# Seven-product gates of a graph recurrence: one part moved, one given its own bank, one load asked for sooner

## The chip, the core and the metric

The kernel runs on one core of one Trainium2 chip. The metric is the device time of one execution in microseconds, the median of several. TensorE (PE) multiplies and transposes into PSUM, used here as eight banks of 128 x 512 fp32; VectorE (DVE) and ScalarE (ACT) read the banks and work in SBUF; SyncE (SP) issues most DMAs. The engines run their own instruction lists in order and wait for each other by semaphores.

## The reference: what is computed

The first layer is a mean aggregation over a 2048 x 2048 adjacency with dense layers; the second is a recurrence of five steps over the same adjacency, cut to what matters:

```python
state = prop_state
for _ in range(N_STEPS):                       # 5
    s_in = state @ in_W.T + in_b
    s_out = state @ out_W.T + out_b
    a_in = Af @ s_in
    a_out = AfT @ s_out
    a = jnp.concatenate([a_in, a_out, state], axis=-1)
    r = jax.nn.sigmoid(a @ r_W.T + r_b)
    z = jax.nn.sigmoid(a @ z_W.T + z_b)
    joined = jnp.concatenate([a_in, a_out, r * state], axis=-1)
    h_hat = jnp.tanh(joined @ h_W.T + h_b)
    state = (1.0 - z) * state + z * h_hat
```

The state is 2048 nodes x 256 features.

## The kernel before

**Tiling and names.** The state lies transposed in `ST` as two feature tiles of 128 by 2048 nodes. Nodes are taken as two pairs of blocks of 512 nodes. One unit n is one pair in one step of the recurrence: n = -2 and -1 (`FIRST` and `FIRST + 1`) are the first and the second pair of step one, n = 0 and 1 those of step two, and so on to 7. u = n + 2 counts the units, p = n % 2 is the pair. The program runs for each n: from n = 0 on two product stages (x = 0, 1), then three gates j = 0 (r), 1 (z), 2 (h).

**Seven products.** The 2 x 2 block product of a gate (two feature tiles by two node blocks) is computed as seven products M1 to M7, called parts, each of three fp32 matmul steps of 128 x 128 by 128 x 512 (`part`); each step appears as two instructions in the trace, so a part is six. Four banks a, b, c, d serve a gate; a gate uses banks 0 to 3 or 4 to 7 in turn, as g = 5n + 2 + j is even or odd. Products accumulate on one another: M1 then M2 in a, M5 then M3 in c, M6 then M7 then M4 in b. Between them the engines take out what they need: ACT copies M1 (`m1_buf`) before M2 may be added, and M5 before M3; DVE adds the bias terms to the tiles of `buf` (two scalar_tensor_tensor for one tile, a pair, L1282 and L1285, `add_bias`), reads M6 out of b (L1295) before M7, and M6 + M7 (`u3`, L1306) before M4. The semaphore `part_ready` counts the parts done (7 per gate), `part_act` ACT's two copies, `part_dve` nine DVE steps per gate (the third is the sum of M6, the ninth u3), `value_ready` the four finished tiles. ACT squashes each tile when its value is ready (L908). After the values of gate 0 DVE multiplies r by the state (L1239, `reset_times_state`), in gate 1 it forms four reset sums (L1214 to L1219, `reset_sums`, semaphore `reset_ready`), which gate 2 waits for.

**Order of the parts.** In most gates PE runs M1, M5, M6, M2, M7, M3, M4 (`GATE`). For the gate n = -1, j = 0 the order is written out apart (`LATE`): M1, M5, M2, M3, transposes, M6, M7, M4, because its sums XT2 to XT4 of the right-hand sides are made late by DVE (`first_sums`, L1161 to L1164).

**Fresh leaves.** In gate 0 of a second pair PE transposes the first pair's new state into the four banks of the gate before (`turn_fresh`, 16 transposes, L489). ACT copies three of them and writes their fp16 high parts (`leaf_first`, L739), DVE forms the low parts (`leaf_low`, L1135, called splits here) and four sums (`leaf_sums`, L1117 to L1122), and ACT the high parts of these. Gate 1 of the same unit writes into the banks which the transposes used, and so waits for `leaf_act` and `leaf_sum`. DVE's order in this gate: bias of tile 1; M6; bias of tiles 3, 2, 0; three splits; u3; tile 2; leaf sums; M3 into tile 1; four splits; two r times state; M4 into tile 3.

**Streamed blocks.** From n = 0 on `product` multiplies fp16 leaves (`LF`) by adjacency blocks of 1 MB, which SP loads from `quad_d` in the order `LOADS` (M1, M6, M5, M2, M7, M3, M4) into six slots. The first three are requested early. Block 3 (M2 of n = 0) and all behind it are requested after `node_ready` has reached 8, the last new state of n = -1. Slot 3 lies at 120 KB, where `first_XS` lies, the state sums that the third matmul step of gates 0 and 1 reads in the first two units. In the first products (x = 0, p = 0) the order on PE is M1, half of M6, half of M5, M2, the other halves, M7, M3, M4, with leaf transposes between them; each product is 16 matmuls, each half 8.

Of the kernel before, what the change touches and what calls it, by code (L numbers as in the profile page):

```python
# [8 lines left out]
ALU = mybir.AluOpType  # L9
# [14 lines left out]
M1, M2, M3, M4, M5, M6, M7 = range(7)  # L24
PLAIN = (M1, M6, M5, M2, M7, M3, M4)
EARLY = (M1, M2, M6, M5, M7, M3, M4)
LATE = (M1, M5, M2, M3, M6, M7, M4)
GATE = (M1, M5, M6, M2, M7, M3, M4)
FIRST = -2
LOADS = (M1, M6, M5, M2, M7, M3, M4)  # L30
# [14 lines left out]
def graph_net(nc, x, adj, w_in, w_out, wg_t, w0_t, w_comb, w_o, cols, b_comb, o2_b, consts, out):  # L45

    ctx = ExitStack()
    with ctx:
# [3 lines left out]
        def sem(name):  # L52
            return ctx.enter_context(nc.semaphore(name))
# [139 lines left out]
        value_ready, squashed = sem("value_ready"), sem("squashed")  # L193
        rs2_ready, kept_ready = sem("rs2_ready"), sem("kept_ready")
        own_ready, reset_ready = sem("own_ready"), sem("reset_ready")
        moved, node_ready = sem("moved"), sem("node_ready")
        leaf_ready, leaf_act, leaf_sum = sem("leaf_ready"), sem("leaf_act"), sem("leaf_sum")
        leaf_hi, leaf_lo = sem("leaf_hi"), sem("leaf_lo")
# [42 lines left out]
        def _(sp):  # L241
# [52 lines left out]
            for k in range(14 * 2 * (STEPS - 1)):  # L294
                n, y, i = k // 14, k // 7 % 2, k % 7
                if k == 3:
                    sp.wait_ge(node_ready, 8)
                if k >= SLOTS:
                    o = k - SLOTS
                    sp.wait_ge(prod_ready, 7 * (o // 7) + place(o // 14, o // 7 % 2, LOADS[o % 7]) + 1)  # L300
                sp.dma_start(slot[k % SLOTS][:, :, :], quad_d[y, n % 2, LOADS[i]]).then_inc(ld_slot[k % SLOTS], 16)
# [20 lines left out]
        def _(pe):  # L322
            ident = cst[:, C_ID:C_ID + P]

            def mm(o, l, r, start, stop, again=False):
                return pe.matmul(o, l, r, start=start, stop=stop, skip_group_check=again)  # L326
# [231 lines left out]
            def gate_group(n, j, last_step):  # L558
# [14 lines left out]
                    third = {M1: r_state[:, 0, :], M2: r_state[:, 3, :], M3: r_state[:, 2, :],  # L573
                             M4: rt4[:, :], M5: r_state[:, 1, :], M6: rt2[:, :], M7: rt3[:, :]}

                def part(op, o):
                    for k in range(FT):
                        mm(o[:, :], W7[:, op, j, k, :], right[op][:, k, :], k == 0 and op in (M1, M5, M6), False, True)
                    mm(o[:, :], W7[:, op, j, 2, :], third[op], False, True, True).then_inc(part_ready, 1)

                def turn_fresh():
# [34 lines left out]
                if n == FIRST + 1 and j == 0:  # L616
                    part(M1, a)
                    pe.wait_ge(own_ready, 4 * u + 4)
                    part(M5, c)
                    pe.wait_ge(part_act, 2 * done + 1)  # L620
                    part(M2, a)
                    pe.wait_ge(part_act, 2 * done + 2)
                    part(M3, c)
                    turn_fresh()
                    pe.wait_ge(x_ready, 4 * u + 2)
                    part(M6, b)
                    pe.wait_ge(x_ready, 4 * u + 4)
                    pe.wait_ge(part_dve, PARTS * done + AT_U2)
                    part(M7, b)
                    pe.wait_ge(part_dve, PARTS * done + AT_U3)  # L630
                    part(M4, b)
                    return
                part(M1, a)
                if j == 0:
# [297 lines left out]
        def _(dve):  # L932
# [327 lines left out]
            def gate_group(n, j, last_step):  # L1260
                p = n % 2
                g = 5 * n + 2 + j
                a, b, c, d = half_banks(g)
                done = 3 * (n - FIRST) + j
                buf = bufs_of(n)[j]
                m1, u3 = m1_buf[:, g % 2, :], u3_buf[:, :]
                n1 = slice(2 * p * BN, 2 * p * BN + BN)
                n2 = slice((2 * p + 1) * BN, (2 * p + 1) * BN + BN)
                fresh_here = j == 0 and p == 1 and not last_step
                tail = j == 2 and p == 1 and not last_step  # L1270
                parts = [PARTS * done]

                def step(ins):
                    parts[0] += 1
                    ins.then_inc(part_dve, 1)

                def own_wait():
                    dve.wait_ge(part_dve, parts[0])

                def add_bias(o, i, f, nodes):  # L1280
                    t = 2 * j + f
                    step(v.scalar_tensor_tensor(out=o, in0=degA_all[:, nodes], scalar=gcol[:, 0, t:t + 1],  # L1282
                                                in1=i, op0=ALU.mult, op1=ALU.add))
                    own_wait()
                    return v.scalar_tensor_tensor(out=o, in0=degT_all[:, nodes], scalar=gcol[:, 1, t:t + 1],  # L1285
                                                  in1=o, op0=ALU.mult, op1=ALU.add)

                def ready(op):
                    dve.wait_ge(part_ready, 7 * done + gate_place(n, j, op) + 1)

                dve.wait_ge(part_act, 2 * done + 1)
                step(add_bias(buf[:, 1, :], m1, 0, n2))
                ready(M6)
                own_wait()
                step(v.tensor_tensor(buf[:, 1, :], b[:, :], buf[:, 1, :], ALU.add))  # L1295
                assert parts[0] == PARTS * done + AT_U2
                step(add_bias(buf[:, 3, :], m1, 1, n1))
                dve.wait_ge(part_act, 2 * done + 2)
                step(add_bias(buf[:, 2, :], buf[:, 2, :], 1, n2))
                ready(M2)  # L1300
                add_bias(buf[:, 0, :], a[:, :], 0, n1).then_inc(value_ready, 1)
                if fresh_here:
                    leaf_low(n + 1, 0, 3)
                ready(M7)
                own_wait()
                step(v.tensor_tensor(u3, b[:, :], m1, ALU.add))  # L1306
                assert parts[0] == PARTS * done + AT_U3 == PARTS * (done + 1)
                own_wait()
                v.tensor_tensor(buf[:, 2, :], u3, buf[:, 2, :], ALU.add).then_inc(value_ready, 1)
                if j == 1:  # L1310
                    reset_sums(n)
                if fresh_here:
                    leaf_sums(n + 1, half_banks(g - 1)[3])
                if j == 2:
                    renew(n, 0)
                ready(M3)
                v.tensor_tensor(buf[:, 1, :], c[:, :], buf[:, 1, :], ALU.add).then_inc(value_ready, 1)
                if fresh_here:
                    leaf_low(n + 1, 3, 7)
                if j == 0:  # L1320
                    reset_times_state(n, 0, 2)
                if j == 2:
                    renew(n, 1)
                if tail:
                    leaf_low(n + 2, 0, 1)
                if n == FIRST and j == 2:
                    own_sums(n + 1)
                ready(M4)
                v.tensor_tensor(buf[:, 3, :], b[:, :], buf[:, 3, :], ALU.add).then_inc(value_ready, 1)
                if j == 2:  # L1330
                    renew(n, 2)
                    renew(n, 3)
                if n == FIRST and j == 2:
                    first_sums(n + 1)
# [97 lines left out]
```

## Time and profile before

| | |
|---|---|
| median of 3 runs | 1252.18 us (1252.12 to 1252.78) |
| profiled execution | 1251.93 us, span 1250.1 us |
| granted TensorE clock, mean | 0.994 |
| TensorE | 1226.1 us busy, 98% of the span |
| VectorE | 761.6 us, 61% |
| ScalarE | 286.9 us, 23% |
| blocks streamed into the slots | 112 of 1024 KB, median 5.1 us to landing |

The span is the time from the first to the last instruction of the profiled execution. Idle time of an engine counts only where it lies on the chain of work that ends last. That chain is 88% TensorE.

### The profile page before, as it was taken

The page shows a single profiled execution, that of the slowest core. Times are in us where ns is not written, and L with a number is a line of the kernel's source. Part 1 is how long each engine was busy: PE and PEld are TensorE (multiplying, and loading weights), DVE is VectorE, ACT ScalarE, POOL GpSimd, SP SyncE. Part 2 cuts the span into 40 slices and gives each one's busy share as a digit, 9 for nine tenths or more (in the row PEclk, how much of TensorE's full clock was granted, in tenths as well). Part 3 has the DMA queues.
Part 4 walks back from the last instruction along what each step waited for, and adds up shares of the span by engine and source line. Part 5 has one row for each costly group of instructions (what it writes and reads, how often), then busy time and mean ns, then how long its engine had stood idle before and what let it go on. Part 6 is the DMA issues. An engine that isn't in the chain of part 4 may idle for free.

```text
span 1250.1 us, 12880 instructions
## 1 busy us (share of the span) xinstructions
PE 1226.1 (98%) x4886; PEld 596.3 (48%) x4886; DVE 761.6 (61%) x1276; ACT 286.9 (23%) x556; POOL 3.0 (0%) x9
## 2 busy tenths in 40 slices
PE   7999999999899999999999999999999999999998
PEld 5666654444344444444444444444444444444445
DVE  5677662796876366278537438735734863662674
ACT  4755300012223012022202103311211330120121
POOL 0000000000000000000000000000000000000000
PEclk9899999999999999999999999999999999999999
DMA  8454460980004911830560480083076029116202
GB/s 307 140 169 164 185 270 37 353 323 1 1 0 190 345 38 48 305 118 0 224 247 1 147 304 21 34 298 139 1 247 224 1 85 352 35 40 229 89 1 68
DMA packets 44506, 180.61 MB, mean 144 GB/s; under 512 B 3489, under 2 KB 13474, under 8 KB 29346
## 3 DMA queue, kind: packets, MB, share of 16 engines
q1 hardware_dynamic: 43440, 176.04, 39.0%
q0 software_dynamic: 720, 3.67, 0.8%
q8 instruction: 36, 0.59, 0.2%
q14 instruction: 20, 0.16, 0.0%
q10 hardware_dynamic: 290, 0.14, 0.0%
HBM read 144.71 MB, written 35.13 MB: 144 GB/s over the span
## 4 chain that ended last, share of the span: by engine, by line
PE 88%; DVE 1%; issue 0%; ACT 0%; DVEq 0%
PE bank L326 86%; PE bank L489 1%; DVE LF L1135 0%; DVE GR L1282 0%; PE bank L442 0%; DVE GR L1285 0%; DVE H L1040 0%; PE bank L395 0%; DVE DR L1008 0%; DVE AT L997 0%; DVE fresh_S L1119 0%; DVE fresh_L L1117 0%; DVE GR L1295 0%; DVE res L1393 0%; DVE stat L947 0%
## 5 line engine op out<-in xcount | busy, mean ns | idle before, releaser
L326 PE MATMUL bank<-slot,LF 128*128 128x512 f16 x1792 | 389.5, 379 | 1.7 <-DVE LF L1135 1.7
L326 PEld LDWEIGHTS bank<-slot,LF 128*128 128x128 f16 x1792 | 175.1, 98 | 212.2 <-issue 4.4
L326 PE MATMUL bank<-X,W 128*128 128x512 f32 x384 | 180.5, 592 | 0.0
L326 PE MATMUL bank<-XT,W 128*128 128x512 f32 x288 | 135.3, 592 | 0.0
L326 PEld LDWEIGHTS bank<-X,W 128*128 128x128 f32 x384 | 72.5, 190 | 88.0 <-issue 86.8
L326 PE MATMUL bank<-AT,SN 128*128 (+1 forms) x256 | 97.1, 379 | 0.0
L326 PE MATMUL bank<-A,SN 128*128 (+1 forms) x256 | 97.0, 379 | 0.0
L1181 DVE TENSOR_TENSOR u_buf<-bank,m_buf 128x512 f32<-128x512 f32 x16 | 11.1, 691 | 134.0 <-PE bank L326 134.0
L326 PEld LDWEIGHTS bank<-XT,W 128*128 128x128 f32 x288 | 54.7, 190 | 68.9 <-issue 68.2
L739 ACT ACTIVATE m_buf<-bank 128x512 f32<-128x512 f32 x46 | 27.4, 595 | 232.0 <-PE bank L326 232.0
L326 PE MATMUL bank<-DR,work 128*128 128x512 f16 x256 | 65.7, 379 | 3.0 <-DVE DR L1008 3.0
L326 PE MATMUL bank<-XS,W 128*128 128x512 f32 x128 | 65.4, 592 | 0.0
L326 PE MATMUL bank<-ST,W 128*128 128x512 f32 x120 | 61.3, 592 | 0.0
L908 ACT ACTIVATE GR<-GR,col 128x512 f32<-128x512 f32 x40 | 28.8, 721 | 99.7 <-DVE GR L1285 54.0
L326 PE MATMUL bank<-first_X,W 128*128 128x512 f32 x96 | 45.3, 594 | 0.0
L908 ACT ACTIVATE GZ<-GZ,col 128x512 f32<-128x512 f32 x32 | 23.1, 722 | 85.6 <-DVE GZ L1285 55.3
L908 ACT ACTIVATE GH<-GH,col 128x512 f32<-128x512 f32 x32 | 23.1, 722 | 85.5 <-DVE GH L1285 56.4
L326 PE MATMUL bank<-GR,W 128*128 128x512 f32 x80 | 40.9, 592 | 0.0
L326 PE MATMUL bank<-first_XT,W 128*128 128x512 f32 x72 | 35.8, 621 | 4.7 <-DVE u_buf L1306 3.8
L739 ACT ACTIVATE A<-WG 128x512 f16<-128x512 int32 x64 | 39.5, 620 | 0.3 <-DMA WG<-in_adj 0.2
L326 PEld LDWEIGHTS bank<-A,SN 128*128 (+1 forms) x256 | 25.0, 98 | 29.9
L326 PEld LDWEIGHTS bank<-AT,SN 128*128 (+1 forms) x256 | 25.0, 98 | 29.7
(209 smaller groups left out, 1412.5 us busy)
## 6 DMA issues: line engine op xcount, KB each, us to landing
slot<-quad_d SPq DMA_DIRECT2D x112, 1024.0 KB, 5.1
WG<-in_adj SPq DMA_DIRECT2D x32, 512.0 KB, 4.2
quad_d<-AT SPq DMA_DIRECT2D x12, 1024.0 KB, 5.0
quad_d<-A SPq DMA_DIRECT2D x12, 1024.0 KB, 9.5
quad_d<-spare SPq DMA_DIRECT2D x4, 1024.0 KB, 4.0
SN<-in_x SPq DMA_DIRECT2D x2, 1024.0 KB, 10.4
x_d<-SN POOLq DMA_DIRECT2D x4, 512.0 KB, 2.9
x1o<-x_d SPq DMA_DIRECT2D x1, 2048.0 KB, 8.1
```

The source lines that it names most:

```text
L326: return pe.matmul(o, l, r, start=start, stop=stop, skip_group_check=again)
L489: last = pe.transpose(o[:, q * P:q * P + P], ST[:, f, n0:n0 + P], ident)
L739: return nc.scalar.activation(o, i, ACT.Copy, scale=scale, **kw)
L908: nc.scalar.activation(buf[:, tile, :], buf[:, tile, :], ACT.Tanh if j == 2 else ACT.Sigmoid, bias=col[:, 10 + 2 * j + f:11 + 2 * j + f]). ...
L1181: v.tensor_tensor(u3, b[:, :], m1, ALU.add).then_inc(prod_dve, 1)
```

## The change

In the gate n = -1, j = 0 the part M3 is issued between M6 and M7 instead of ahead of the transposes, and M4 goes into bank d with a start flag of its own. M7 waits for eight DVE steps instead of three, the eighth being the sum of M6; M4 waits for no DVE step. DVE does the bias additions of tiles 3, 2 and 0 ahead of the sum of M6, does the leaf sums before it waits for M7, adds the products of M7 to tile 3 (one more instruction, semaphore `late_sum`), and adds M4 from bank d. In SP's list block 3 waits for 35 parts, that is, for the end of gate 1 of n = -1, and block 4 for `node_ready` 8. All other gates and units keep their order.

```diff
--- before.py
+++ after.py
@@ -24,7 +24,7 @@
 M1, M2, M3, M4, M5, M6, M7 = range(7)
 PLAIN = (M1, M6, M5, M2, M7, M3, M4)
 EARLY = (M1, M2, M6, M5, M7, M3, M4)
-LATE = (M1, M5, M2, M3, M6, M7, M4)
+LATE = (M1, M5, M2, M6, M3, M7, M4)
 GATE = (M1, M5, M6, M2, M7, M3, M4)
 FIRST = -2
 LOADS = (M1, M6, M5, M2, M7, M3, M4)
@@ -193,6 +193,7 @@
         value_ready, squashed = sem("value_ready"), sem("squashed")
         rs2_ready, kept_ready = sem("rs2_ready"), sem("kept_ready")
         own_ready, reset_ready = sem("own_ready"), sem("reset_ready")
+        late_sum = sem("late_sum")
         moved, node_ready = sem("moved"), sem("node_ready")
         leaf_ready, leaf_act, leaf_sum = sem("leaf_ready"), sem("leaf_act"), sem("leaf_sum")
         leaf_hi, leaf_lo = sem("leaf_hi"), sem("leaf_lo")
@@ -294,6 +295,8 @@
             for k in range(14 * 2 * (STEPS - 1)):
                 n, y, i = k // 14, k // 7 % 2, k % 7
                 if k == 3:
+                    sp.wait_ge(part_ready, 7 * 5)
+                if k == 4:
                     sp.wait_ge(node_ready, 8)
                 if k >= SLOTS:
                     o = k - SLOTS
@@ -573,9 +576,10 @@
                     third = {M1: r_state[:, 0, :], M2: r_state[:, 3, :], M3: r_state[:, 2, :],
                              M4: rt4[:, :], M5: r_state[:, 1, :], M6: rt2[:, :], M7: rt3[:, :]}
 
-                def part(op, o):
+                def part(op, o, alone=False):
                     for k in range(FT):
-                        mm(o[:, :], W7[:, op, j, k, :], right[op][:, k, :], k == 0 and op in (M1, M5, M6), False, True)
+                        mm(o[:, :], W7[:, op, j, k, :], right[op][:, k, :],
+                           k == 0 and (alone or op in (M1, M5, M6)), False, True)
                     mm(o[:, :], W7[:, op, j, 2, :], third[op], False, True, True).then_inc(part_ready, 1)
 
                 def turn_fresh():
@@ -619,16 +623,15 @@
                     part(M5, c)
                     pe.wait_ge(part_act, 2 * done + 1)
                     part(M2, a)
-                    pe.wait_ge(part_act, 2 * done + 2)
-                    part(M3, c)
                     turn_fresh()
                     pe.wait_ge(x_ready, 4 * u + 2)
                     part(M6, b)
+                    pe.wait_ge(part_act, 2 * done + 2)
+                    part(M3, c)
                     pe.wait_ge(x_ready, 4 * u + 4)
-                    pe.wait_ge(part_dve, PARTS * done + AT_U2)
+                    pe.wait_ge(part_dve, PARTS * done + PARTS - 1)
                     part(M7, b)
-                    pe.wait_ge(part_dve, PARTS * done + AT_U3)
-                    part(M4, b)
+                    part(M4, d, True)
                     return
                 part(M1, a)
                 if j == 0:
@@ -1288,33 +1291,48 @@
                 def ready(op):
                     dve.wait_ge(part_ready, 7 * done + gate_place(n, j, op) + 1)
 
+                def products_of(op):
+                    return {M2: a, M3: c, M4: d if late else b, M6: b, M7: b}[op][:, :]
+
+                late = n == FIRST + 1 and j == 0
                 dve.wait_ge(part_act, 2 * done + 1)
                 step(add_bias(buf[:, 1, :], m1, 0, n2))
+                if late:
+                    step(add_bias(buf[:, 3, :], m1, 1, n1))
+                    dve.wait_ge(part_act, 2 * done + 2)
+                    step(add_bias(buf[:, 2, :], buf[:, 2, :], 1, n2))
+                    ready(M2)
+                    add_bias(buf[:, 0, :], products_of(M2), 0, n1).then_inc(value_ready, 1)
                 ready(M6)
                 own_wait()
-                step(v.tensor_tensor(buf[:, 1, :], b[:, :], buf[:, 1, :], ALU.add))
-                assert parts[0] == PARTS * done + AT_U2
-                step(add_bias(buf[:, 3, :], m1, 1, n1))
-                dve.wait_ge(part_act, 2 * done + 2)
-                step(add_bias(buf[:, 2, :], buf[:, 2, :], 1, n2))
-                ready(M2)
-                add_bias(buf[:, 0, :], a[:, :], 0, n1).then_inc(value_ready, 1)
+                step(v.tensor_tensor(buf[:, 1, :], products_of(M6), buf[:, 1, :], ALU.add))
+                if not late:
+                    assert parts[0] == PARTS * done + AT_U2
+                    step(add_bias(buf[:, 3, :], m1, 1, n1))
+                    dve.wait_ge(part_act, 2 * done + 2)
+                    step(add_bias(buf[:, 2, :], buf[:, 2, :], 1, n2))
+                    ready(M2)
+                    add_bias(buf[:, 0, :], products_of(M2), 0, n1).then_inc(value_ready, 1)
                 if fresh_here:
                     leaf_low(n + 1, 0, 3)
+                if late:
+                    leaf_sums(n + 1, half_banks(g - 1)[3])
                 ready(M7)
                 own_wait()
-                step(v.tensor_tensor(u3, b[:, :], m1, ALU.add))
+                step(v.tensor_tensor(u3, products_of(M7), m1, ALU.add))
                 assert parts[0] == PARTS * done + AT_U3 == PARTS * (done + 1)
                 own_wait()
                 v.tensor_tensor(buf[:, 2, :], u3, buf[:, 2, :], ALU.add).then_inc(value_ready, 1)
+                if late:
+                    v.tensor_tensor(buf[:, 3, :], products_of(M7), buf[:, 3, :], ALU.add).then_inc(late_sum, 1)
                 if j == 1:
                     reset_sums(n)
-                if fresh_here:
+                if fresh_here and not late:
                     leaf_sums(n + 1, half_banks(g - 1)[3])
                 if j == 2:
                     renew(n, 0)
                 ready(M3)
-                v.tensor_tensor(buf[:, 1, :], c[:, :], buf[:, 1, :], ALU.add).then_inc(value_ready, 1)
+                v.tensor_tensor(buf[:, 1, :], products_of(M3), buf[:, 1, :], ALU.add).then_inc(value_ready, 1)
                 if fresh_here:
                     leaf_low(n + 1, 3, 7)
                 if j == 0:
@@ -1326,7 +1344,9 @@
                 if n == FIRST and j == 2:
                     own_sums(n + 1)
                 ready(M4)
-                v.tensor_tensor(buf[:, 3, :], b[:, :], buf[:, 3, :], ALU.add).then_inc(value_ready, 1)
+                if late:
+                    dve.wait_ge(late_sum, 1)
+                v.tensor_tensor(buf[:, 3, :], products_of(M4), buf[:, 3, :], ALU.add).then_inc(value_ready, 1)
                 if j == 2:
                     renew(n, 2)
                     renew(n, 3)
```

## Rows read from the trace of the kernel before

**Rows 1.** The page: TensorE busy over the whole span.

```profile
PE 1226.1 (98%) x4886; PEld 596.3 (48%) x4886; DVE 761.6 (61%) x1276; ACT 286.9 (23%) x556; POOL 3.0 (0%) x9
```

**Rows 2.** Waits of PE, 316 to 420: line, waited for, us, times, longest.

```profile
PE bank L326 <- DVE u_buf L1306: 3.8, 1, 3.8
PE bank L326 <- DVE LF L1135: 1.7, 1, 1.7
PE bank L326 <- DVE GR L1295: 0.9, 1, 0.9
```

**Rows 3.** Timeline 316 to 350: start us, us, engine, line, operation, out<-in, count.

```profile
320.38 1.88 PE L326 MATMUL bank<-first_X,W 128*128 128x512 f32 x4
...
328.10 1.88 PE L326 MATMUL bank<-first_X,W 128*128 128x512 f32 x4
...
329.45 0.75 DVE L1282 SCALAR_TENSOR_TENSOR GR<-DR,gcol,m_buf 128x512 f32<-128x512 f16 x1
...
332.42 1.88 PE L326 MATMUL bank<-first_XT,W 128*128 128x512 f32 x4
...
335.20 0.69 DVE L1295 TENSOR_TENSOR GR<-bank,GR 128x512 f32<-128x512 f32 x1 [4.22 <-PE bank L326]
...
335.81 0.74 DVE L1282 SCALAR_TENSOR_TENSOR GR<-DR,gcol,m_buf 128x512 f32<-128x512 f16 x1
...
336.04 1.96 PE L326 MATMUL bank<-first_XT,W 128*128 128x512 f32 x4 [0.88 <-DVE GR L1295]
...
340.15 1.89 DVE L1135 SCALAR_TENSOR_TENSOR LF<-fresh_L,LF 128x512 f16<-128x512 f32 x3
...
342.69 3.78 PE L326 MATMUL bank<-first_XT,W 128*128 128x512 f32 x4 [3.84 <-DVE u_buf L1306]
...
343.28 0.68 DVE L1117 TENSOR_TENSOR fresh_L<-bank,fresh_L 128x512 f32<-128x512 f32 x1
...
346.53 0.68 DVE L1135 SCALAR_TENSOR_TENSOR LF<-fresh_S,LF 128x512 f16<-128x512 f32 x1
```

**Rows 4.** Timeline 346 to 384, gate j = 1.

```profile
347.97 2.05 PE L326 MATMUL bank<-first_X,W 128*128 128x512 f32 x4
...
350.14 0.68 DVE L1329 TENSOR_TENSOR GR<-bank,GR 128x512 f32<-128x512 f32 x1
...
351.49 0.58 ACT L739 ACTIVATE m_buf<-bank 128x512 f32<-128x512 f32 x1
...
352.22 0.75 DVE L1282 SCALAR_TENSOR_TENSOR first_GZ<-DR,gcol,m_buf 128x512 f32<-128x512 f16 x1
...
361.22 0.69 DVE L1306 TENSOR_TENSOR u_buf<-bank,m_buf 128x512 f32<-128x512 f32 x1
...
364.61 0.68 DVE L1219 TENSOR_TENSOR RT<-GR,first_RT 128x512 f32<-128x512 f32 x1
...
366.17 1.88 PE L326 MATMUL bank<-first_X,W 128*128 128x512 f32 x4
```

**Rows 5.** Stretches: length, PE busy, the other engines, granted clock, DMA share, GB/s.

```profile
336.00:339.00 3.00, 2.81 (x6) 1.06 (x6) 2.93 (x5) 0.00 (x0) 0.00 (x0) 1.00 0.00 0
...
339.00:342.00 3.00, 0.00 (x0) 0.00 (x0) 2.96 (x6) 0.72 (x1) 0.00 (x0) 0.91 0.00 0
...
343.00:346.00 3.00, 3.00 (x4) 1.20 (x4) 2.93 (x6) 2.00 (x4) 0.00 (x0) 0.50 0.00 0
```

**Rows 6.** Timeline 388 to 398; landing times of the blocks requested.

```profile
389.92 1.99 SPq L301 DMA_DIRECT2D slot<-quad_d  x4
...
391.28 1.89 PE L326 MATMUL bank<-slot,LF 128*128 128x512 f16 x8
...
394.85 3.40 PE L326 MATMUL bank<-slot,LF 128*128 128x512 f16 x15 [1.68 <-DVE LF L1135]
...
DMA to landing us min/median/max: 4.8/7.9/10.9
```

**Rows 7.** Timeline 592 to 612, the same products one step later.

```profile
601.62 10.74 PE L326 MATMUL bank<-slot,LF 128*128 128x512 f16 x49
```

## The prediction, made before the changed kernel was run

> **What bounds the kernel now.** I read the page first: TensorE is busy 1226 us of a span of 1250 [rows 1], so a change pays only where it takes idle or slow time from TensorE. The waits of TensorE around the change are three [rows 2]: 3.8 us for the vector engine's u3 (L1306), 1.7 us put down to a leaf split (L1135), 0.9 us for the sum of M6 (L1295). The timeline [rows 3, 4] shows where they lie. In the first gate of the second pair (n = -1, j = 0; M1 starts at 320.38) three parts take 328.10 - 320.38 = 7.72 us, 2.573 each; the 16 transposes follow M3 and end 1.74 us later, at 332.42, where M6 starts. At 336.04 M7 starts, 1.05 us after M6 gave TensorE free (332.42 + 2.57 = 334.99). M7 is issued by 338.61, and M4 starts at 342.69, 4.08 us late. M4 then takes 347.97 - 342.69 = 5.28 instead of 2.57, since the granted clock is 0.50 there (the 1.2 GHz level), having fallen in the 3.84 us of idleness [rows 5]. The next gate (j = 1) takes 366.17 - 347.97 = 18.20 us for seven parts worth 18.01, the last 0.19 of the low clock. So 1.05 + 4.08 + 2.71 + 0.19 = 8.0 us lie here beyond the matmuls' own time, and about 1.8 more lie at the first products.
>
> **The sequence after the change, TensorE up to M7.** M1, M5 and M2 keep their places and end at 328.10. M3 leaves, so the transposes run from 328.10 to 329.84, M6 to 332.42 (DVE writes its operand XT2 ahead of the bias additions, which start at 329.45, [rows 3]), M3 to 334.99. The transposes need the first pair's new states, finished before those additions as well. Nothing is paid for this exchange, it fills the time that DVE needs.
>
> **VectorE up to M7.** The additions start at 329.45 as before. In the row, three pairs take 340.15 - 335.81 = 4.34 us, 1.447 a pair [rows 3]. Now four pairs stand in a row ahead of the sum of M6: 329.45 + 4 x 1.447 = 335.24. M6 itself is ready at about 332.6, so the sum is held by VectorE and starts at 335.24, practically where it did before (335.20). From that sum's start to M7 is 336.04 - 335.20 = 0.84, so M7 starts at 336.08, a wait of 1.09 us, 0.04 more than now. The gap at M7 is not removed.
>
> **M4 in bank d.** It no longer waits for u3. It starts at 336.08 + 2.57 = 338.65 and ends at 341.22. That takes away the 4.08 us, and, as no long gap is left, the 2.71 + 0.19 of the low clock. The trace shows no M4 that opens a bank; M1 opens one in each gate and costs the same 2.57, so I take nothing for it (bounds: 0 to the 0.04 by which my part lengths are uncertain). At the end of the gate the gain is 347.97 - 341.22 = 6.75 us.
>
> **What VectorE now has in front of the next gate.** Nothing of its work went away and one addition came (tile 3 plus the products of M7, 0.61 us by the step 335.20 to 335.81). Three leaf splits take 1.89; the four leaf sums 2.65 (343.28 to 346.53 holds five instructions, less one of 0.61) [rows 3]. So: sum of M6 335.24, splits 335.85, leaf sums from 337.77, when the last split is done, to 340.5 (337.77 + 2.65 and 0.07 of a last instruction's end). Gate j = 1 writes the banks that the transposes used and waits for these sums; TensorE comes at 341.22, 0.7 later, so nothing is paid. u3 starts at 340.4, value 1 at 341.1, the new addition 341.75, the sum of M3 342.4. The next four splits wait for ScalarE: a sigmoid and a copy of some 0.6 to 0.7 us each (351.49 - 350.14 - 0.68 is 0.67, the copy itself 0.58, [rows 4]) behind value 1, so 343.15. From that split to the sum of M4 is 350.14 - 346.53 = 3.61: 346.8, where M4 was ready long before (341.4). That is 5.6 us behind the start of j = 1; now it is 350.14 - 347.97 = 2.2. VectorE is late by 3.4 us relative to TensorE, and this is where a new wait can come.
>
> **Gate j = 1.** The sum of M4 to the copy of M1 is 351.49 - 350.14 = 1.35: the copy ends at 346.8 + 1.35 + 0.58 = 348.7. TensorE wants it for M2 at 341.22 + 3 x 2.573 = 348.94: free by 0.2. The first addition starts 352.22 - 350.14 = 2.08 behind the sum of M4, at 348.9, the sum of M6 at 350.35, M7 could start at 351.2 and its turn is 351.5: free by 0.3. Three pairs and a step later, 350.35 + 0.61 + 4.34 = 355.3, u3 starts and ends at 356.0; M4's turn is 356.66: free. The last of the reset sums ends 364.61 + 0.68 - 361.22 = 4.07 behind u3's start [rows 4], at 359.35; j = 2 waits for it, and its turn is 341.22 + 18.01 = 359.23. Here 0.1 to 0.2 us of waiting appear, where now 0.9 are free (365.29 against 366.17). I take j = 2 at 359.45; the bounds are 359.23 and, if each of VectorE's handovers costs 0.1 more, 359.95. Gain at that point: 366.17 - 359.45 = **6.7 us** (6.2 to 6.9). In j = 2 VectorE waits for matmuls again, so no lag is carried on.
>
> **The fourth block.** At the first products (n = 0) the half of M5 starts at 391.28 and M2 at 394.85 [rows 6]. Eight matmuls of 0.216 are 1.73, so M2 is 1.84 us late. The wait is put down to L1135, but the code of M2 wants the leaf splits up to the tenth, which is that of L12, and not the later one, of a leaf sum, that ended just before 394.85; and in the next step the same sequence runs 49 matmuls without a gap from 601.62, with the same leaf chain beside it [rows 7]. What differs here is block 3, requested at 389.92, when the state is ready, and the quickest of these transfers took 4.8 us to land: 394.72. So it is the block. Asked for after 35 parts, that is at the end of j = 1 (about 359.4, slot 3 being the bytes of first_XS, whose last reader is that M4), it has some 23 us until 383 (389.92 less the gain of 6.7), more to M2. It lands beneath j = 2; SP has nothing else to request until the state is ready, and the DMA share is 0.00 in each stretch of [rows 5]. On SP's queue only the wait for block 4 stands behind it, whose condition comes 24 us later. Block 4 becomes the first of the burst; M7 wants it two products after M2's turn, so about 393.0 + 6.9 = 399.9 on the old clock, against a landing near 394.7. What is late next are the leaf splits of M6's second half: 394.83 against the end of M2 at 393.01 + 3.45 = 396.46, free by 1.6. Gain **1.84 us** (bounds 0, if it were the split after all, and 1.84).
>
> **Sum.** 6.7 + 1.84 = 8.55 us. Behind that the chain is TensorE alone, so it arrives in full. The profiled execution took 1251.93 us (span 1250.1, 1.8 around it); it becomes 1243.4, span 1241.55. It lies 0.25 below the median of the runs, 1252.18, so I forecast a median of **1243.6**.
>
> **Rivals.**
> 1. **The load is not the limit at M2** (the split is). Then only 6.7 come: 1245.5. For it speaks the releaser named in rows 2, against it the step-two sequence. Chance 0.05.
> 2. **The clock falls in the gap before M7.** The gap of 1.09 us stays. If the clock fell there, M7 and M4 would run at 0.50, as M4 does now, for the 2.7 + 0.2 us that it costs now: 1246.5. Against it: the same gap of 1.05 us with the same matmuls before it left the clock at 1.00 in 336:339, and it fell only in the idle stretch of 339:342 [rows 5]. Chance 0.05. The Trainium skill, "TensorE: Matmul & The Clock Gate", Part 4: PE-mode transpose, says that transposes don't count as busy in the way that matmuls do; and its section A second HAM failure mode: psum-queue depth-cycling says that small idle gaps between groups that cycle through banks can make the clock oscillate. Both speak against this order, which has transposes, a gap and one more bank; by them the time would be this rival's. The trace speaks for less: before the change the transposes lie nearer to that gap and the clock held.
> 3. **VectorE is the bound of j = 1 and j = 2** rather than a neighbour: the lag of 3.4 us costs 0.2 to 0.5 at M2, M7 and at the start of j = 2 together some 1 us: 1244.6. For it speaks that its queue is full from 329.45 on, against it that each of my margins is positive but one. Chance 0.09.
> 4. **Slower than before.** The clock falls before M7 and stays low, since the gates keep having small gaps (M2, M7, the start of j = 2). Each matmul instruction at half speed costs 0.43 us more, so 20 of them beyond the saving, some 17 us at the low clock, eat the 8.55; past that it is slower. If it held for j = 1 and j = 2 whole it would be 36 - 8.6 = 27 us slower, 1280. In the rows now it was back for nearly all of j = 1, which took 18.20 us instead of 18.01, so 0.01.
>
> The forecast has 0.80. **Range**: the bounds of the terms give 8.77 to 8.0, 1243.4 to 1244.2; with rivals 1 and 3 and 0.7 for the scatter of the runs (1252.12 to 1252.78) it is 1242.6 to 1246.0. This kernel's measurement can tell about 0.2%, 2.5 us, from no change. Faster by more than that 0.98 (all cases but the last and mixtures of them), within it 0.01, slower 0.01.
>
> **What would show it.** M4 right behind M7 and the clock at 1.00 through 340 to 350; M7 still about 1.1 us late, released by L1295 (or its new line); start of j = 1 at 341.2, of j = 2 at 359.4 with a small wait for L1219; block 3 issued near 359.4 and M2 of n = 0 without a gap. Wrong would be a larger gap at M7 (the additions taking more than 1.45 a pair against the copies), a clock at 0.50 in that stretch, or a gap at M2 of n = 0 with the block landed.

## The result

The changed kernel takes **1244.37 us** (median of four runs, 1243.72 to 1245.34) against 1252.15 before (1251.26 to 1252.78): ratio 0.9939, 95% interval 0.9922 to 0.9956. The forecast was 1243.6, range 1242.6 to 1246.0. The profiled execution took 1245.34 us, span 1243.5. Run again on another occasion, five times beside nine runs of the kernel before, the two stood at 1245.46 and 1253.37, ratio 0.9940 (0.9927 to 0.9954).

The page's line on the engines, the answer to [rows 1]: TensorE is busy for 1.6 us less and the span is shorter by 6.6, so most of the gain is idle time.

```profile
PE 1224.5 (98%) x4886; PEld 596.1 (48%) x4886; DVE 762.2 (61%) x1277; ACT 286.3 (23%) x556; POOL 3.0 (0%) x9
```

The waits of TensorE between 316 and 420 us (line, waited for, us in total, times, longest), the answer to [rows 2]:

```profile
PE bank L329 <- DVE GR L1308: 0.9, 1, 0.9
PE bank L329 <- DVE RT L1222: 0.2, 1, 0.2
```

The long wait for u3 (3.8) and the one at the first products (1.7) are gone, the one of 0.9 us at M7 stays, and a new one of 0.2 us for the last reset sum has come. In the timeline of the changed kernel, which answers [rows 3, 4] (start us, us, engine, line, operation):

```profile
322.06 1.88 PE L329 MATMUL bank<-first_X,W 128*128 128x512 f32 x4
...
331.14 0.74 DVE L1285 SCALAR_TENSOR_TENSOR GR<-DR,gcol,m_buf 128x512 f32<-128x512 f16 x1
...
336.93 0.68 DVE L1308 TENSOR_TENSOR GR<-bank,GR 128x512 f32<-128x512 f32 x1
...
337.76 1.96 PE L329 MATMUL bank<-first_XT,W 128*128 128x512 f32 x4 [0.91 <-DVE GR L1308]
...
340.41 1.88 PE L329 MATMUL bank<-first_XT,W 128*128 128x512 f32 x4
...
342.18 0.68 DVE L1322 TENSOR_TENSOR u_buf<-bank,m_buf 128x512 f32<-128x512 f32 x1
...
342.99 1.88 PE L329 MATMUL bank<-first_X,W 128*128 128x512 f32 x4
...
348.52 0.68 DVE L1349 TENSOR_TENSOR GR<-bank,GR 128x512 f32<-128x512 f32 x1
...
351.38 0.75 DVE L1288 SCALAR_TENSOR_TENSOR first_GZ<-H,gcol,first_GZ 128x512 f32<-128x512 f16 x1
...
352.24 0.69 DVE L1308 TENSOR_TENSOR first_GZ<-bank,first_GZ 128x512 f32<-128x512 f32 x1
...
357.19 0.68 DVE L1322 TENSOR_TENSOR u_buf<-bank,m_buf 128x512 f32<-128x512 f32 x1
...
360.57 0.69 DVE L1222 TENSOR_TENSOR RT<-GR,first_RT 128x512 f32<-128x512 f32 x1
...
361.40 1.95 PE L329 MATMUL bank<-first_X,W 128*128 128x512 f32 x4 [0.22 <-DVE RT L1222]
```

M7 starts at 337.76, M4 stands right behind it at 340.41, while u3 (L1322) starts only at 342.18, and the next gate starts at 342.99. The gate j = 2 starts at 361.40.

To compare executions, I count from the first matmul of M1 in the gate n = -1, j = 0, at 320.38 before and at 322.06 here, since up to there both kernels issue the same work:

| from the gate's first matmul, us | before | changed | forecast |
|---|---|---|---|
| M7 | 15.66 | 15.70 | 15.70 |
| M4 | 22.31 | 18.35 | 18.27 |
| gate j = 1 | 27.59 | 20.93 | 20.84 |
| gate j = 2 | 45.79 | 39.34 | 39.07 |
| last instruction | 925.67 | 917.45 | 917.12 |

(The last instruction starts at 1246.05 before and 1239.51 now.) So the change is worth 8.22 us. The profiled execution shows 6.6 because it came to the gate 1.68 us later. That difference is older than the change, in the start of the kernel. The stretch 40 to 50 us, before and then changed (length, busy us of PE, PEld, DVE, ACT, POOL, granted clock, DMA share, GB/s):

```profile
40.00:50.00 10.00, 10.00 (x99) 5.93 (x99) 5.80 (x19) 8.72 (x29) 0.00 (x0) 1.00 0.67 214
```

```profile
40.00:50.00 10.00, 9.98 (x85) 5.71 (x86) 5.01 (x16) 7.54 (x25) 0.00 (x0) 0.83 0.57 184
```

A clock of 0.83 over ten us is 1.7 us of work not done. It goes with the execution and not with the change: among the profiles of the experiments below, the kernel before with M3 moved has 0.86 in this stretch and the changed kernel with late leaf sums 1.00. The nine runs of before of the second occasion fit this: four lie at 1252.0 to 1252.4 with mean clocks of 0.994 and 0.995, five at 1253.4 to 1253.9 with 0.992 and 0.993, and none between.

The granted clock in the gate, which answers [rows 5]:

```profile
336.00:339.00 3.00, 2.09 (x5) 0.70 (x5) 2.96 (x6) 0.72 (x1) 0.00 (x0) 1.00 0.00 0
...
339.00:342.00 3.00, 3.00 (x8) 1.33 (x7) 2.83 (x5) 0.00 (x0) 0.00 (x0) 1.00 0.00 0
...
342.00:345.00 3.00, 3.00 (x8) 1.33 (x7) 2.85 (x6) 1.38 (x3) 0.00 (x0) 1.00 0.00 0
```

It stays at 1.00 (2.4 GHz) over the gap of 0.91 us and behind it; before it fell to 0.50 (1.2 GHz) in the idle stretch ahead of M4.

At the first products, the answer to [rows 6], and the request of block 3:

```profile
361.21 0.32 SPq L304 DMA_DIRECT2D slot<-quad_d  x1
...
385.23 1.27 SPq L304 DMA_DIRECT2D slot<-quad_d  x3
...
386.58 5.78 PE L329 MATMUL bank<-slot,LF 128*128 128x512 f16 x26
...
389.44 0.68 DVE L1138 SCALAR_TENSOR_TENSOR LF<-fresh_S,LF 128x512 f16<-128x512 f32 x1
```

The half of M5 and M2 behind it are one row of matmuls from 386.58 on, with no gap. M2 starts at 386.58 + 8 x 0.216 = 388.31, a microsecond before the split L1138, to which the wait was put down before, even begins (389.44). SP requests three blocks here instead of four; the fourth was requested at 361.21, when the last part of j = 1 was done.

### The profile page after: what moved, and what is told of

Its sections match the earlier page's. It is cut to its first block, busy times and chain, and to the rows that moved or that the text cites. A ratio compares the mean times of both kernels' runs of the same rounds, so it can differ in the third digit from the quotient of the medians.

```text
span 1243.5 us, 12882 instructions
## 1 busy us (share of the span) xinstructions
PE 1224.5 (98%) x4886; PEld 596.1 (48%) x4886; DVE 762.2 (61%) x1277; ACT 286.3 (23%) x556; POOL 3.0 (0%) x9
## 4 chain that ended last, share of the span: by engine, by line
PE 85%; DVE 3%; issue 1%; ACT 0%; DVEq 0%
PE bank L329 84%; PE bank L492 1%; DVE LF L1138 0%; DVE GR L1285 0%; DVE first_GZ L1285 0%; DVE first_GH L1258 0%; DVE first_GZ L1288 0%; DVE GR L1288 0%; DVE ST L1261 0%; DVE u_buf L1322 0%; DVE GR L1242 0%; PE bank L445 0%; ACT GR L911 0%; DVE H L1043 0%; DVE first_XT L1166 0%
## 5 line engine op out<-in xcount | busy, mean ns | idle before, releaser
L329 PEld LDWEIGHTS bank<-XS,W 128*128 128x128 f32 x128 | 24.3, 190 | 30.6 <-issue 30.6
```

## The experiments

The experiments are compared by the distances from the gate's first matmul, which repeat to 0.05 us in four kernels that were profiled twice, where medians of four to ten runs scatter by one (the changed kernel profiled a second time: 15.71, 18.36, 20.94, 39.36 and 917.49).

| kernel | M7 | M4 | j = 1 | j = 2 | last | median, ratio to the kernel before as run beside it (interval) |
|---|---|---|---|---|---|---|
| before | 15.66 | 22.31 | 27.59 | 45.79 | 925.67 | |
| changed | 15.70 | 18.35 | 20.93 | 39.34 | 917.45 | 1244.37, 0.9939 (0.9922 to 0.9956) |
| changed, late request | 15.71 | 18.36 | 20.94 | 39.35 | 919.31 | 1246.93, 0.9949 (0.9932 to 0.9965) |
| before, early request | 15.66 | 22.32 | 27.60 | 45.68 | 923.74 | 1250.47, 0.9983 (0.9973 to 0.9992) |
| changed, M4 in bank b | 15.70 | 20.86 | 25.23 | 43.26 | 921.31 | 1249.04, 0.9964 (0.9950 to 0.9978) |
| changed, M3 in its old place | 15.71 | 18.36 | 20.94 | 39.36 | 917.48 | 1244.84, 0.9937 (0.9920 to 0.9954) |
| changed, leaf sums late | 15.71 | 18.36 | 23.37 | 43.16 | 921.22 | 1247.57, 0.9958 (0.9941 to 0.9974) |
| before, M3 moved | 14.62 | 19.74 | 23.21 | 41.31 | 921.21 | 1248.40, 0.9967 (0.9956 to 0.9979) |
| changed, sum of M6 sooner | 14.62 | 17.20 | 20.64 | 39.63 | 917.77 | 1245.58, 0.9940 (0.9923 to 0.9957) |
| less ahead of the next gate | 14.63 | 17.20 | 19.78 | 37.93 | 915.99 | 1243.33, 0.9926 (0.9910 to 0.9943) |

### The request of block 3, undone and alone

```diff
-                if k == 3:
-                    sp.wait_ge(part_ready, 7 * 5)
-                if k == 4:
+                if k == 3:
                     sp.wait_ge(node_ready, 8)
```

> The changed kernel, but block 3 is requested behind the last new state again, as before the change. Times are counted from the first matmul of M1 in the gate n = -1, j = 0 (changed kernel: j = 2 starts at 39.34, last instruction at 917.45; before: 45.79 and 925.67). Theory (the landing of block 3 releases M2 of the first products): M2 waits again, 1.8 us, last instruction at 919.2, some 0.14% slower than the changed kernel. Rival (the leaf split releases it, and the change of order removed that): no wait, 917.45.

Measured: 919.31, 1.86 more than the changed kernel; up to j = 2 nothing differs. The wait is back, and put down to the split again (first products of this kernel):

```profile
385.21 2.08 SPq L302 DMA_DIRECT2D slot<-quad_d  x4
...
386.57 1.89 PE L327 MATMUL bank<-slot,LF 128*128 128x512 f16 x8
...
389.43 0.68 DVE L1136 SCALAR_TENSOR_TENSOR LF<-fresh_S,LF 128x512 f16<-128x512 f32 x1
...
390.12 2.10 PE L327 MATMUL bank<-slot,LF 128*128 128x512 f16 x9 [1.66 <-DVE LF L1136]
...
DMA to landing us min/median/max: 4.8/7.9/10.9
```

The order of splits, transposes and products is that of the changed kernel, only the request is later: 385.21 + 4.8 = 390.0, and M2 starts at 390.12. The split ends at 390.11 by chance. In the changed kernel M2 did not wait for it, so it is the block.

> The kernel before with the early request alone. Theory: j = 2 starts at 45.79 as before, M2 of the first products follows the half of M5 without a gap, last instruction at 925.67 - 1.84 = 923.8. Rival (the split): 925.67, the wait stays and is released by the same split.

The other way round (the two lines of the change alone put into the kernel before): 923.74, 1.93 less, of which 0.11 was there before j = 2 starts (45.68 for 45.79; the clock was back a little sooner in j = 1). The request is worth 1.8 us with either order of the gate. Both expectations of the theory hold, the rival falls.

### M4 in bank b again

```diff
-                    part(M4, d, True)
+                    pe.wait_ge(part_dve, PARTS * done + AT_U3)
+                    part(M4, b)
...
-                return {M2: a, M3: c, M4: d if late else b, M6: b, M7: b}[op][:, :]
+                return {M2: a, M3: c, M4: b, M6: b, M7: b}[op][:, :]
...
-                if late:
-                    v.tensor_tensor(buf[:, 3, :], products_of(M7), buf[:, 3, :], ALU.add).then_inc(late_sum, 1)
...
-                if late:
-                    dve.wait_ge(late_sum, 1)
```

> The changed kernel, but M4 goes on in bank b behind u3, and the addition of M7 to tile 3 is gone. Theory: u3 ends 20.8 after the gate's start, M4 starts at 20.85 instead of 18.35 (a gap of 2.5 us), j = 1 at 23.4, and as TensorE is then behind VectorE, j = 2 at 41.5: 2.1 us over the changed kernel if the clock stays at 1.00 in a gap of 2.5 us. Rival (the clock falls in this gap as it did in 4.1 us): M4 takes up to 5.3 us, 5 us over the changed kernel, so that the own bank was worth most of the gain by the clock alone.

Measured: M4 at 20.86, as expected, but j = 1 at 25.23, j = 2 at 43.26, last 921.31: 3.86 us over the changed kernel, neither 2.1 nor 5. The timeline of TensorE and the clock around it:

```profile
337.81 1.96 PE L329 MATMUL bank<-first_XT,W 128*128 128x512 f32 x4 [0.92 <-DVE GR L1309]
...
342.97 3.28 PE L329 MATMUL bank<-first_XT,W 128*128 128x512 f32 x4 [2.34 <-DVE u_buf L1323]
...
346.04 1.46 PE L329 MATMUL bank<-first_XS,W 128*128 128x512 f32 x2
...
347.34 1.88 PE L329 MATMUL bank<-first_X,W 128*128 128x512 f32 x4
```

```profile
341.00:343.00 2.00, 0.03 (x1) 0.03 (x1) 1.94 (x4) 0.00 (x0) 0.00 (x0) 1.00 0.00 0
...
343.00:345.00 2.00, 2.00 (x3) 0.91 (x4) 1.29 (x3) 1.33 (x3) 0.00 (x0) 0.63 0.00 0
...
345.00:347.00 2.00, 2.00 (x4) 0.77 (x3) 2.00 (x4) 2.00 (x4) 0.00 (x0) 0.52 0.00 0
```

M4 took 347.34 - 342.97 = 4.37 instead of 2.57: the clock fell behind a gap of 2.34 us (1.00 in 341 to 343, then 0.63 and 0.52), which my theory had not expected, and it was low for less long than in the kernel before. So the bank alone is worth 3.9 us: 2.5 of waiting and 1.8 of clock, less 0.4 of waiting at j = 2 that is not needed then. Profiled again, it gave 20.86, 25.21, 43.23 and 921.30:

> M4 in bank b, again, for its clock around the gap of 2.34 us, where it fell. Theory (differs between executions): 921.3 from the gate's first matmul to the last instruction, or down to 919.5 with the clock at 1.00. Rival (fixed by the order of work, here two gaps in a row): 921.3 again.

It is the same to 0.03, though this execution came to the gate 1.53 us sooner (320.58 for 322.11). The rival of this run holds in these two executions: the fall and its price come with the order of work. Its moment does not: in the first execution M4 starts at 342.97 and the clock is still 1.00 in 343.0 to 343.5 and 0.51 in 343.5 to 344.0; in the second M4 starts at 341.44 and the clock is 0.92 in 341.0 to 341.5 and 0.50 in 341.5 to 342.0, so it fell as M4 started, half a microsecond sooner.

### M3 in its old place

```diff
                     part(M2, a)
+                    pe.wait_ge(part_act, 2 * done + 2)
+                    part(M3, c)
                     turn_fresh()
                     pe.wait_ge(x_ready, 4 * u + 2)
                     part(M6, b)
-                    pe.wait_ge(part_act, 2 * done + 2)
-                    part(M3, c)
```

(`LATE` with it.)

> The changed kernel, but M3 stands ahead of the transposes again. Theory (the sum of M6 starts when the four pairs of additions are done, and M6 is ready before that in either order): M6 ends 14.6 after the gate's start, the sum starts at 14.87, M7 at 15.70 as in the changed kernel, total the same within 0.1 us. Rival (M3 behind M6 is what covers the wait for the sum): M7 starts up to 2.5 us later, total 1 to 2.5 us longer.

Measured: 15.71 and 917.48, the theory to 0.03. In the changed kernel the move of M3 brings nothing, since all four pairs of additions stand ahead of the sum of M6 anyway, and M7 waits for them in either order.

### Leaf sums behind u3 again

```diff
-                if late:
-                    leaf_sums(n + 1, half_banks(g - 1)[3])
                 ready(M7)
...
-                if fresh_here and not late:
+                if fresh_here:
                     leaf_sums(n + 1, half_banks(g - 1)[3])
```

> The changed kernel, but the leaf sums come behind u3 and its two additions again. Times from the first matmul of M1 in the gate n = -1, j = 0. Theory: u3 starts at 18.55 (when M7 is done), the leaf sums run from 20.5 to 23.2, j = 1 waits for them and starts at 23.25 instead of 20.93, j = 2 at about 41.3 instead of 39.34: 2 us over the changed kernel. Rival (the next gate is released by something else, and VectorE has the same work in either order): j = 2 within 0.5 us of 39.34.

Measured: j = 1 at 23.37 (expected 23.25), so it is these sums that the next gate waits for; but j = 2 at 43.16, 3.8 us over the changed kernel instead of 2. The gate j = 1 took 43.16 - 23.37 = 19.79 where its parts need 18.02. The waits of this kernel, and its clock behind them:

```profile
PE bank L329 <- DVE fresh_L L1125: 2.3, 1, 2.3
PE bank L329 <- DVE GR L1308: 0.9, 1, 0.9
```

```profile
343.00:345.00 2.00, 1.17 (x3) 0.68 (x4) 2.00 (x5) 2.00 (x5) 0.00 (x0) 1.00 0.00 0
...
345.00:347.00 2.00, 2.00 (x3) 0.67 (x2) 2.00 (x4) 0.19 (x1) 0.00 (x0) 0.50 0.00 0
```

The clock fell again, this time 1.2 us after TensorE had gone on (343.83), to 0.50 in 345 to 347, behind idle stretches of 0.92 and 2.27 us. The theory named the right release, but it put the price at 2 us, about half of what was measured, because it left out the clock.

### M3 moved alone in the kernel before

The edit of the fourth kernel the other way round, in the kernel before.

> The kernel before with M3 moved between M6 and M7 alone (M4 in bank b, additions behind the sum of M6, late request). Theory: the sum of M6 runs under M3, M7 starts at 14.6 without a gap, u3 ends at 19.7, M4 starts at 19.75 with a gap of 2.6 us; with the clock at 1.00 the gate j = 1 starts at 23.1 (behind the leaf sums), j = 2 at 41.2, last instruction at 921.1, 4.6 under the kernel before. Rival (the clock falls in a gap of 2.6 us): some 2.9 us more, 924.0.

Measured: M7 at 14.62 without a gap, M4 at 19.74, j = 1 at 23.21, j = 2 at 41.31, last 921.21. The theory holds throughout, and the clock stayed at 1.00 although the gap is 2.38 us, longer than the two behind which it fell:

```profile
336.52 1.88 PE L326 MATMUL bank<-first_XT,W 128*128 128x512 f32 x4
...
341.64 1.98 PE L326 MATMUL bank<-first_XT,W 128*128 128x512 f32 x4 [2.38 <-DVE u_buf L1306]
...
345.11 1.96 PE L326 MATMUL bank<-first_X,W 128*128 128x512 f32 x4 [0.63 <-DVE fresh_L L1122]
```

```profile
339.00:341.00 2.00, 0.26 (x1) 0.00 (x0) 2.00 (x5) 0.72 (x1) 0.00 (x0) 1.00 0.00 0
...
341.00:343.00 2.00, 1.36 (x3) 0.68 (x4) 1.93 (x4) 0.65 (x1) 0.00 (x0) 1.00 0.00 0
...
343.00:345.00 2.00, 1.48 (x4) 0.38 (x2) 1.97 (x4) 1.40 (x4) 0.00 (x0) 1.00 0.00 0
```

> M3 moved alone, again, for its clock in the gap of 2.38 us ahead of M4, where it stayed at 1.00. Theory (whether the clock falls in a gap of about 2.3 to 2.4 us differs between executions of one kernel): the last instruction lies 921.2 behind the gate's first matmul, or up to 3.6 more. Rival (it is fixed by the kernel's order of work): 921.2 again.

Again: 19.75, 23.22, 41.32, 921.22, the clock at 1.00. Both executions came to the gate at nearly the same moment (321.90 and 321.97), so the two alone don't exclude that the moment decides. The times of the seven runs do: the profiled one took 1248.94 with the gate at 321.90, that is 5.83 beyond 321.90 + 921.21, and the two shortest, 1247.57 and 1247.66, then put the gate at about 320.5 if the clock held. Had it fallen there, at a price of 1.8, the gate would have come at 318.8, and no profile here has it before 320.38. What differs from the two kernels where it fell is what TensorE did before the gap: here it was unbroken up to it, there it had been idle for 0.92 us one or two parts earlier. That this earlier gap is what tips it is the reading that fits; no run changes it alone.

So the same move that is worth nothing in the changed kernel is worth 4.5 us alone (925.67 - 921.21): M4 starts 2.57 us sooner, the gate needs 3.47 us from there instead of 5.28, since the clock stays up, and j = 1 takes 18.10 instead of 18.20.

### The gap at M7, taken away

```diff
                 if late:
                     step(add_bias(buf[:, 3, :], m1, 1, n1))
-                    dve.wait_ge(part_act, 2 * done + 2)
-                    step(add_bias(buf[:, 2, :], buf[:, 2, :], 1, n2))
-                    ready(M2)
-                    add_bias(buf[:, 0, :], products_of(M2), 0, n1).then_inc(value_ready, 1)
                 ready(M6)
...
                 step(v.tensor_tensor(buf[:, 1, :], products_of(M6), buf[:, 1, :], ALU.add))
+                if late:
+                    dve.wait_ge(part_act, 2 * done + 2)
+                    step(add_bias(buf[:, 2, :], buf[:, 2, :], 1, n2))
+                    ready(M2)
+                    add_bias(buf[:, 0, :], products_of(M2), 0, n1).then_inc(value_ready, 1)
```

M7 waits for step 5 instead of step 8.

> The changed kernel, but VectorE takes the sum of M6 behind two pairs of additions instead of four, so that it runs under M3. Theory (VectorE's queue, not the gap at M7, sets the start of j = 2): M7 starts at 14.6, the gap of 1.1 us is gone, j = 1 waits for the leaf sums until 20.4, and j = 2 starts at 39.3 to 39.6, no sooner than in the changed kernel: total the same or 0.2 longer. Rival (what TensorE gains stays gained): j = 2 at 38.3, 1.05 us less.

Measured: M7 at 14.62, the gap of 1.08 us gone, and j = 2 at 39.63, 0.29 later than in the changed kernel; last 917.77. Its waits show where the 1.08 us went:

```profile
PE bank L329 <- DVE fresh_L L1125: 0.7, 1, 0.7
PE bank L329 <- DVE RT L1222: 0.3, 1, 0.3
```

j = 1 starts 0.87 us later than M4's end would allow (17.20 + 2.57 = 19.77 against 20.64), and from j = 1 to j = 2 it is 18.99 us where 18.02 are the parts' own: 0.97 lost, against 0.39 in the changed kernel. All of the 1.08 is given back, and 0.3 more. Of the 0.97 us, 0.51 are ahead of j = 2 and 0.29 ahead of M2 of j = 1, which starts at 350.83 behind ScalarE's copy of M1 (ended at 350.78); the rest is in the first instructions behind the gaps. The 0.3 are VectorE's own: it now waits 0.18 us for M6, and its splits start at 15.75 (337.86) instead of 15.47 (337.53). The theory holds, with sizes a little short (20.4 and at most 39.6 were expected). VectorE's queue from the additions to the last reset sum is the bound: in the changed kernel it is busy for 29.1 of these 30.1 us, and its one wait for another engine is 0.19 us, for a sigmoid of ScalarE. A gap of TensorE inside it costs nothing as long as the clock holds.

### Less of VectorE's work ahead of the next gate

On top of the kernel before this one: the splits and leaf sums stand ahead of the pairs of tiles 2 and 0, and behind the reset sums of j = 1 go two of the late splits and the addition of u3 to tile 2.

```diff
+                if j == 1 and n == FIRST + 1:
+                    reset_sums(n)
                 v.tensor_tensor(buf[:, 2, :], u3, buf[:, 2, :], ALU.add).then_inc(value_ready, 1)
...
-                    leaf_low(n + 1, 3, 7)
+                    leaf_low(n + 1, 3, 5 if late else 7)
+                if j == 1 and n == FIRST + 1:
+                    leaf_low(n + 1, 5, 7)
```

> As the run before, and VectorE has less ahead of the start of j = 2: leaf splits and sums before the last two pairs, two of the four late splits and the tile addition of u3 in j = 1 behind the reset sums. Theory (VectorE's queue is the bound): with about 1.9 us less in front of the reset sums TensorE keeps the gap it gained: j = 1 starts at 19.8, j = 2 at 37.8 to 38.0 instead of 39.34, total 1.4 us under the changed kernel. Rival: the wait moves to M2 or M7 of j = 1, and less than half of it arrives.

Measured: j = 1 at 19.78, j = 2 at 37.93, last 915.99, 1.46 us under the changed kernel. No wait of TensorE is listed between 316 and 420 us any more, and TensorE runs through from M1 on; from j = 1 to j = 2 it needs 18.15 us, 0.13 over the parts' own:

```profile
336.76 1.88 PE L329 MATMUL bank<-first_XT,W 128*128 128x512 f32 x4
...
341.91 1.88 PE L329 MATMUL bank<-first_X,W 128*128 128x512 f32 x4
...
360.06 1.88 PE L329 MATMUL bank<-first_X,W 128*128 128x512 f32 x4
```

The repetition, on one chip with the changed kernel:

> The changed kernel as it is, beside its better version on the same chip, and as a second profile. Theory (all of the gain lies in the gate n = -1, j = 0 to the first products, and the scatter of single executions, 1243.7 to 1245.3, lies ahead of the gate): from the gate's first matmul to the last instruction 917.4 to 917.5 again, whatever the execution's own time; the gate starts at 320.4 to 322.1. Rival (the scatter is in the changed part): that stretch differs by up to 1.7 us.

> The version with less ahead of the next gate, again, on the chip of the run before. Theory: 916.0 from the gate's first matmul to the last instruction, and a median 1.4 us under the changed kernel's. Rival (the difference of 1.0 us between the medians of four runs was scatter): medians within 0.3 us.

Measured: the changed kernel 917.49 with the gate at 321.30, median 1245.46; this version 915.99 with the gate at 322.79, median 1243.75 (1242.08 to 1244.74), ratio 0.9923 (0.9910 to 0.9937). By the trace it is 1.5 us faster; the medians differ by 1.7 side by side, and by 1.0 between the two occasions on which the first runs were taken. The distances repeat (917.45 and 917.49, 915.99 twice) while the gate's start moves by 0.8 and 0.7 us, so the scatter is ahead of the gate.

## Why the prediction was right, point by point

- **VectorE up to M7.** Right: four pairs end where the sum of M6 started before; M7 at 15.70 as forecast, its gap not removed. That the exchange with M3 costs and brings nothing was right too (917.48 with M3 in its old place).
- **M4 in bank d.** Right, 18.35 for 18.27: the first instructions of M7 behind the gap take 0.08 longer (340.41 - 337.76 = 2.65 for 2.57). The 2.71 + 0.19 of low clock went with it.
- **VectorE in front of j = 1.** Right: j = 1 starts unhindered; the sum of M4 stands at 26.46 (348.52), forecast 26.42. The run with the leaf sums late shows the cost if they are not moved, 3.8 us.
- **Gate j = 1.** The place was right, the size too small: 0.2 us of waiting forecast, 342.99 + 18.02 = 361.01 to 361.40 is 0.39. The term that was mis-sized is the step from the last bias addition to the sum of M6. I took 0.67, the step between independent instructions; here the sum reads the tile that the addition has just written, and the rows show 352.24 - 351.38 = 0.86, with M6 done at 350.71, so that TensorE did not hold it. That 0.19 goes through to the last reset sum; with it j = 2 stands 0.27 later than forecast.
- **The fourth block.** Right: 1.84 forecast, 1.86 by undoing it, 1.77 in the profiles (from j = 2 to the end: 925.67 - 45.79 = 879.88 before, 917.45 - 39.34 = 878.11 now).
- **Sum.** 8.55 forecast, 8.22 found: 0.27 too much up to j = 2, 0.07 at the block. The median lies 0.8 over the forecast; 0.3 of it is this, the rest is within the scatter of the start of the kernel, which the forecast had put to 0.7. The bounds of the terms alone (1243.4 to 1244.2) leave the median out by 0.2; it lies in the range by the allowance for scatter and rivals.
- **Rivals.** The first (the split, not the block) falls by both runs. The second (the clock falls at M7's gap) did not come: in every profile with that gap the clock held at it. The Trainium skill, "TensorE: Matmul & The Clock Gate", Part 4: PE-mode transpose, has transposes not count as busy in the same way. No run here takes them out; the two kernels in which the clock fell later and the changed kernel, in which it held, have the same 16 transposes at the same place. The third (VectorE as the bound) was given too little, 0.09: VectorE is the bound up to j = 2, as the run with M7's gap taken away shows. It waits out only 0.39 us at j = 2 and not the rival's 1 us. The median, 1244.37, is nearer to this rival's 1244.6 than to the forecast's 1243.6, and only the distances tell the two apart. The fourth did not come.
- **What I underrated** without harm: the clock. In the two kernels with a gap of 2.3 us and another shortly before, the gap had a price beyond its length, so the bank and the order of the leaf sums are worth 3.9 and 3.8 us each, not the 2 that their waits alone give. The two overlap, since the whole change is worth 6.45 us up to j = 2. The order of the bias additions was undone only in part, in the run that takes M7's gap away.

## What to carry to other kernels

Look for the queue that runs through a stretch without a pause (here VectorE's, from the bias additions to the last reset sum): a gap of another engine inside it is free as long as it doesn't cost the clock, and closing it brings nothing until work is taken out of the queue ahead of the next hand-over. A wait put down to the engine that ended last may be a DMA's: compare with a later stretch of the same code in which the DMA had time. When the time before the changed place scatters, compare distances from a common instruction, not medians.

## What the runs showed of the hardware

The clock of TensorE fell from 1.00 to 0.50 behind a gap of 2.34 us (twice) and of 2.27 us when TensorE had already been idle for 0.92 us one or two parts before, at a price of 1.8 us each. It fell as the matmuls went on, 0.5 us later and 1.2 us later, in the three executions; it stayed at 1.00 through 2.38 us with 0.63 us behind it (twice) when the work before was unbroken. The Trainium skill, "TensorE: Matmul & The Clock Gate", section A second HAM failure mode: psum-queue depth-cycling, describes a clock that goes down and up again where TensorE idles briefly and often between groups of matmuls. These two kernels are not that case: each has two gaps and one fall. They don't speak against it, and they show a fall with far fewer gaps. How much idleness together is too much, these runs don't settle.
